# A vision tower on one core: GpSimd takes five of eight code masks and half of the high powers

## The reference, cut to what matters

```python
# the filter bank: 64 modes, 1024 times
A = jnp.exp(A_abslog + 1j * A_phase)
dtA = jnp.log(A)
Cc = (C[..., 0] + 1j * C[..., 1]) * (A - 1.0) / dtA
K = jnp.exp(dtA[:, :, None] * t)
h = 2.0 * jnp.einsum('chn,hnl->chl', Cc, K).real

# the coded weights of L0_ffn, 1024 x 1024, 16 codes, one scale for 64 of them
w = NF4_CODE[w_idx.reshape(-1, BLOCK)] * absmax[:, None]
```

## Time and profile before

| | us |
|---|---|
| median of three executions | 4150.96 |
| the profiled execution, first to last instruction | 4148.3 |
| PE busy | 3922.9 (95%) |
| DVE busy | 2708.0 (65%) |
| POOL busy | 2237.8 (54%) |
| ACT busy | 2082.5 (50%) |

### The profile page before, as it was taken

One profiled execution on the slowest core, in us unless ns is written; L12 is line 12 of the kernel. 1 busy time (PEld: TensorE's weight loads), 2 busy tenths in 40 slices (PEclk: granted clock), 3 DMA queues, 4 the chain that ended last, 5 costly groups with the idle time before them and its releaser, 6 DMA issues.

```text
span 4148.3 us, 59709 instructions
## 1 busy us (share of the span) xinstructions
PE 3922.9 (95%) x22920; PEld 2601.4 (63%) x22920; DVE 2708.0 (65%) x2970; ACT 2082.5 (50%) x3052; POOL 2237.8 (54%) x972
## 2 busy tenths in 40 slices
PE   4899999999999999999999999999999999999998
PEld 1568777444768777544577867644477877744466
DVE  6855562999355474699635565499825556389943
ACT  7842344777232344777423234577623224477732
POOL 0023343999533343799733334499843343389962
PEclk7999999999999999999999999999999999999999
DMA  4242233000322223100222223300133223300022
GB/s 111 78 147 77 82 111 108 16 15 15 119 92 82 72 87 124 58 15 15 69 102 97 77 71 120 100 13 16 40 106 97 77 87 102 110 30 15 18 84 71
DMA packets 93817, 303.28 MB, mean 73 GB/s; under 512 B 11520, under 2 KB 15872, under 8 KB 91008
## 3 DMA queue, kind: packets, MB, share of 16 engines
q1 hardware_dynamic: 80320, 275.70, 20.8%
q10 hardware_dynamic: 13248, 24.12, 1.8%
HBM read 255.74 MB, written 44.04 MB: 72 GB/s over the span
## 4 chain that ended last, share of the span: by engine, by line
PE 35%; issue 33%; DVE 20%; POOL 11%; ACT 1%; POOLq 0%; ACTq 0%; DVEq 0%
PE psg L954 20%; DVE sb_wst L1765 17%; POOL sb_wl L528 9%; PE psx L1203 4%; PE psg L1024 3%; POOL sb_wst L567 2%; PE psg L1219 2%; PE psg L1029 1%; PE psx L1251 1%; DVE psg L1738 1%; PE psg L1336 1%; DVE psg L1737 1%; PE psx L971 0%; PE psx L1274 0%; PE psx L1275 0%
## 5 line engine op out<-in xcount | busy, mean ns | idle before, releaser
L528 POOL TENSOR_TENSOR sb_wl<-sb_raw,sb_wh 128x1024 fp32r<-128x1024 f32 x388 | 961.6, 2482 | 1832.0 <-ACT sb_wh L648 1831.7
L1765 DVE TENSOR_TENSOR_SCAN sb_wst<-sb_dA,psx 128x1024 f32<-128x1024 f32 x512 | 1130.1, 2267 | 8.4 <-PE psx L1203 6.1
L790 ACT ACTIVATE sb_dA<-sb_dlt,sb_a_sb 128x504 f32<-128x504 f32 x1024 | 647.0, 705 | 53.0 <-DVE sb_wst L1765 50.8
L648 ACT ACTIVATE sb_wh<-sb_raw 128x1024 fp32r<-128x1024 f32 x388 | 407.3, 1053 | 526.0 <-PE psg L954 219.4
L1203 PEld LDWEIGHTS psx<-sb_dgB,sb_duT 64*128 64x128 f32 x4096 | 359.5, 188 | 462.1 <-DVE sb_wst L1765 322.8
L1203 PE MATMUL psx<-sb_dgB,sb_duT 64*128 64x256 f32 x4096 | 587.1, 406 | 50.1 <-DVE sb_wst L1765 48.5
L1219 PE MATMUL psg<-sb_wst,sb_cst 64*64 64x512 f32 x4096 | 607.2, 618 | 17.3 <-POOL sb_wst L567 16.4
L567 POOL TENSOR_TENSOR sb_wst<-sb_wst,sb_cb_hi 128x1024 f32<-128x1024 f32 x256 | 596.0, 2363 | 29.2 <-DVE sb_wst L1765 29.1
L567 POOL TENSOR_TENSOR sb_wst<-sb_wst,sb_cb_lo 128x1024 f32<-128x1024 f32 x256 | 600.6, 2370 | 9.8 <-DVE sb_wst L1765 9.6
L954 PE MATMUL psg<-sb_xh,sb_wh 128*128 128x512 f32 x2080 | 533.4, 398 | 12.9 <-POOL sb_wl L528 7.4
L954 PE MATMUL psg<-sb_xh,sb_wl 128*128 128x512 f32 x2080 | 515.9, 390 | 0.0
(11 more groups left out here) (283 smaller groups left out, 5059.8 us busy)
## 6 DMA issues: line engine op xcount, KB each, us to landing
sb_raw<-in_w SPq DMA_DIRECT2D x360, 512.0 KB, 3.5
sb_raw<-w_ffn_dequantized SPq DMA_DIRECT2D x32, 512.0 KB, 3.3
gates<-sb_gt ACTq DMA_DIRECT2D x64, 256.0 KB, 2.1
sb_gin<-gates SPq DMA_DIRECT2D x64, 256.0 KB, 2.7
h_after_tok<-sb_h SPq DMA_DIRECT2D x4, 2048.0 KB, 8.7
sb_h<-h_after_tok SPq DMA_DIRECT2D x4, 2048.0 KB, 8.0
out<-sb_h SPq DMA_DIRECT2D x4, 2048.0 KB, 7.2
sb_dqi<-in_w_idx ACTq DMA_DIRECT2D x28, 256.0 KB, 4.2
```

The source lines that it names most:

```text
L528: pool.tensor_tensor(rest(b, i0), raw[:, i0 % RAW, :, :], high(b, i0).bitcast(F32), ALU.subtract).then_inc(s_wl, 1)
L648: A(high(b, i0), raw[:, i0 % RAW, :, :], ACT.Copy).then_inc(s_wh, 1)
L790: ins_ = A(dA[:, (m * NQ + k) % RING, :, n, 1:S], dlt[:, m % 2, :].rearrange("p (b s) -> p b s", b=NB)[:, :, 1:S], ACT.Exp, scale=a_sb[:, ...
L1765: v.tensor_tensor_scan(wst[:, x, 4 * j:4 * j + 4, :, :].rearrange("p b n s -> p (b n s)"), dA[:, x, 4 * j:4 * j + 4, :, :].rearrange("p b ...
```

## The change

GpSimd gets a program of its own in the opening. It makes five of the eight masks of every half (`mkp`, four buffers, one compare each), VectorE two and ScalarE one. GpSimd also makes the four imaginary instructions of `high_` for every group (`high_im`), and `filters(g)` waits for them through `s_ph`. `EARLY` goes from 9 to 14, and the last two halves stand behind filter groups 0 and 1. On VectorE the table's first product now comes ahead of the first masks, and masks stand in the middle of `reduce_turns` too. The loads of codes move from ScalarE's queue to SP's, into the loop that stores the weights. ScalarE keeps two buffers for its masks and one for `away`. Strips 0 and 1 are loaded once the last low powers are made and split ahead of the last group's copies of `hT`; GpSimd makes their rests as soon as all halves are done. To free the space, `dqa` moves within SBUF.

```diff
-RING_ACT, RING_DVE = 3, 4
+RING_ACT, RING_DVE, RING_POOL = 2, 4, 4
-EARLY = 9
-LATE = [[9], [10], [11], [12], [13], [14], [15], []]
-BY_ACT = [4 if i < EARLY else 3 for i in range(HALVES)]
-BY_DVE = [PAIRS - n for n in BY_ACT]
+EARLY = 14
+LATE = [[14], [15], [], [], [], [], [], []]
+BY_DVE, BY_POOL, BY_ACT = 2, 5, 1
...
@@ sync
             for i in range(HALVES):
                 m, q = i // 2, i % 2
+                if i + 2 < HALVES:
+                    sp.wait_ge(s_dqf, i + 1)
+                    load_codes(sp, i + 2)
                 sp.wait_ge(s_dq, i + 1)
...
-            sp.wait_ge(s_hT, S // 2)
+            sp.wait_ge(s_px, S // FG)
...
                         first_strips(0, 0, 2)
+                        sp.wait_ge(s_hT, S // 2)
...
@@ gpsimd
+            def masks(i):
+                pool.wait_ge(s_dqf, i + 1)
+                for j in range(BY_POOL):
+                    at = i * BY_POOL + j
+                    if at >= RING_POOL:
+                        pool.wait_ge(s_usedp, at - RING_POOL + 1)
+                    pool.tensor_scalar(mkp[:, at % RING_POOL, :, :], dqf[:, i % 2, :, :], C("code", BY_DVE + j, 1), None,
+                                       ALU.is_equal).then_inc(s_mkp, 1)
+
+            def high_im(g):
+                a, z = g * FG, (g + 1) * FG
+                pool.wait_ge(s_tab, TAB_COEF)
+                if g >= 2:
+                    pool.wait_ge(s_filt, (g - 1) * FG // 2)
+                for blk in range(NBLK):
+                    ins_ = pool.tensor_tensor(high_[:, g % 2, 1, :, blk, :, :],
+                                              coef[:, 1, a:z, blk * NB:(blk + 1) * NB].unsqueeze(2).to_broadcast([P, FG, KC, NB]),
+                                              tabs[:, 1, a:z, 4:12].unsqueeze(3).to_broadcast([P, FG, KC, NB]), ALU.mult)
+                ins_.then_inc(s_ph, 1)
+
+            for i in range(EARLY):
+                masks(i)
+            for g in range(S // FG):
+                high_im(g)
+                for i in LATE[g]:
+                    masks(i)
+            pool.wait_ge(s_dq, HALVES)
...
@@ scalar, converted
                 if i >= 2:
-                    act.wait_ge(s_mkd, DVE0[i - 1])
+                    act.wait_ge(s_mkd, BY_DVE * (i - 1))
+                    act.wait_ge(s_mkp, BY_POOL * (i - 1))
                 A(dqf[:, q, :, :], dqi[:, q, :, :], ACT.Copy).then_inc(s_dqf, 1)
-                if i + 2 < HALVES:
-                    act.wait_ge(s_dqf, i + 1)
-                    load_codes(act, i + 2)
...
             for g in range(S // FG):
                 for i in LATE[g]:
                     masks(i)
+                if g == S // FG - 1:
+                    act.wait_ge(s_px, S // FG)
+                    act.wait_ge(s_ph, S // FG)
+                    for i in range(2):
+                        split(0, i)
                 copies(g)
...
@@ tensor, filters
                 pe.wait_ge(s_px, g + 1)
+                pe.wait_ge(s_ph, g + 1)
...
@@ vector
-            def reduce_turns(dst, ang, tmp, cols):
+            def reduce_turns(dst, ang, tmp, cols, between=None):
...
                 own.link(stt(dst, tmp, -TURN_HI, ang, ALU.mult, ALU.add))
+                if between is not None:
+                    masks(between)
...
-            masks(0)
             own.link(tt(reg, ph.unsqueeze(2).to_broadcast([P, S, 32]),
                         C("t32").unsqueeze(1).to_broadcast([P, S, 32]), ALU.mult))
-            reduce_turns(tab[:, 0, :, :], reg, reg2, 0)
+            masks(0)
+            reduce_turns(tab[:, 0, :, :], reg, reg2, 0, 1)
...
@@ vector, powers
-                for e in range(2):
-                    for blk in range(NBLK):
-                        tt(high_[:, g % 2, e, :, blk, :, :],
...
+                for blk in range(NBLK):
+                    tt(high_[:, g % 2, 0, :, blk, :, :],
```

More of the change, by code:

```diff
@@ L135 @@
 FG = 8
-EARLY = 9
-LATE = [[9], [10], [11], [12], [13], [14], [15], []]
-BY_ACT = [4 if i < EARLY else 3 for i in range(HALVES)]
-BY_DVE = [PAIRS - n for n in BY_ACT]
-ACT0 = [sum(BY_ACT[:i]) for i in range(HALVES + 1)]
-DVE0 = [sum(BY_DVE[:i]) for i in range(HALVES + 1)]
+EARLY = 14
+LATE = [[14], [15], [], [], [], [], [], []]
+BY_DVE, BY_POOL, BY_ACT = 2, 5, 1
+assert BY_DVE + BY_POOL + BY_ACT == PAIRS
 def pair_parts(p):
@@ L601, in masks @@
                 act.wait_ge(s_dqf, i + 1)
[L602 to L606, removed]
+                for j in range(BY_ACT):
+                    at = BY_ACT * i + j
+                    if at >= 1:
+                        act.wait_ge(s_mka, at)
+                    A(away[:, :, :], dqf[:, q, :, :], ACT.Abs, bias=C("minus", BY_DVE + BY_POOL + j, 1)).then_inc(s_away, 1)
                     act.wait_ge(s_away, at + 1)
@@ L609, in masks @@
                         act.wait_ge(s_useda, at - RING_ACT + 1)
-                    A(mka[:, at % RING_ACT, :, :], away[:, at % 2, :, :], ACT.Relu, bias=C("one"), scale=-1.0).then_inc(s_mka, 1)
+                    A(mka[:, at % RING_ACT, :, :], away[:, :, :], ACT.Relu, bias=C("one"), scale=-1.0).then_inc(s_mka, 1)
             def copies(g):
@@ L635, in _ @@
             A(gco[:, 2, :], mode[:, 0, :], ACT.Exp).then_inc(s_tabA, 1)
-            for i in range(5, EARLY):
+            for i in range(7, EARLY):
                 masks(i)
@@ L676, in _ @@
                         mean_copy(0)
-                    for i in range(AHEAD if b else 2):
-                        split(b, i)
+                    if b:
+                        for i in range(AHEAD):
+                            split(b, i)
                     norm(b, 0)
@@ L1414, in masks @@
                     weights(i - 2)
-                for j in range(BY_DVE[i]):
-                    at = DVE0[i] + j
+                for j in range(BY_DVE):
+                    at = BY_DVE * i + j
                     if at >= RING_DVE:
@@ L1452, in _ @@
             reduce_turns(tabs[:, 0, :, :], reg[:, :, 0:12], reg2[:, :, 0:12], 2)
+            masks(5)
             reduce_turns(tabs[:, 1, :, 0:4], reg[:, :, 0:4], reg2[:, :, 0:4], 3)
@@ L1455, in _ @@
             assert own.n == TAB_SIN[2], own.n
-            masks(3)
+            masks(6)
             for t, col in ((0, 2), (1, 4)):
@@ L1477, in _ @@
             assert own.n == TAB_E, own.n
-            masks(4)
+            masks(7)
             v.wait_ge(s_tabA, 6)
@@ L1482, in _ @@
                 own.link(tt(tab[:, t, :, :], tab[:, t, :, :], etab[:, :, :], ALU.mult))
+            masks(8)
             for t in range(2):
                 own.link(tt(tabs[:, t, :, :], tabs[:, t, :, :], etabs[:, :, :], ALU.mult))
-            masks(5)
             v.wait_ge(s_tabA, 7)
@@ L1509, in _ @@
                 own.link(stt(g2, gim, C("gmix", 4 * e + 3, 1), g2, ALU.mult, ALU.add))
-            masks(6)
+            masks(9)
             v.wait_ge(s_x, 64)
@@ L1521, in _ @@
                 own.link(tt(coef[:, e, :, :], coef[:, e, :, :], x, ALU.add))
-            masks(7)
+                masks(10 + e)
+            assert own.n == TAB_COEF, own.n
             def powers(g):
@@ L1546, in _ @@
             powers(0)
-            masks(8)
+            for i in range(12, EARLY):
+                masks(i)
             for g in range(S // FG):
```

64 lines of the change are left out of this document (36 added, 28 removed).

## The result

| | before | after |
|---|---|---|
| median beside each other, us | 4150.99 (4146.23 to 4151.47) | 4262.41 (4259.99 to 4264.87, 4 runs) |
| profiled span | 4148.3 | 4262.9 |
| first filters | 139.15 | 238.01 |
| mean starts | 232.60 | 340.64 |
| first matmul with `xh` | 242.44 | 348.59 |

The ratio is 1.0267 [1.0254, 1.0279]: slower by 2.7%, against 0.8% forecast and an upper end of 4215. All but some 8 us of the difference of the spans (114.6) is there when the first matmul with `xh` begins (106.15). The rest appears later, in instructions that the change doesn't touch. That later part takes 3902.8 to 3914.4 us in the profiled runs of this document, whatever was edited ahead of it, so a single span can't tell 10 us.

What follows compares the result with a forecast made beforehand. Mask making bounds the first stretch, TensorE the second; with VectorE and GpSimd taking turns, the mean starts 36.9 us later and the strips give -4.0: 4148.3 + 32.9 + 2.7 = 4184 us, slower by 0.8%, range 4120 to 4215.

Steps and rivals of the forecast that it cites:

- VectorE's and GpSimd's turns: Opening: instructions of the two engines exclude each other for their whole length, hiding only 0.13 to 0.14 us at a turn.
- GpSimd's mask: Opening: one GpSimd compare of 128x1024 takes 1.10 us, with ends 0.9 and 2.36.
- a sign of being wrong: GpSimd masks whose minimum is above 1.5 us would show the prediction wrong.
- Until the filters begin: From 13.3 us: GpSimd's turns 68, VectorE 78, waits 7, then products 4.6, so filters(0) starts at 171 us.
- Groups 0 and 1: First two filter groups: the fifth mask waits for TensorE until after the filters, so 19.3 us each, where now 12.
- Groups 2 to 7: Later filter groups: GpSimd's 4.6 and VectorE's 5.7 us make 10.3 each, above TensorE's 7.17.
- SP's loads at nothing: Codes' loads on SP's queue are hidden by two dqi buffers and a pace above 10 us a half.
- TensorE's clock: Opening and filters: costed at nothing, up to +10 us if the clock falls in the filters.
- The strips: First norm: strips 0 and 1 split ahead let it end at 246.1 instead of 250.1, -4.0 us.
- Slow compares: Rival: GpSimd's compare takes 1.9 to 2.36 us, 80 cost 64 to 100 more: 4245 to 4285 us; chance 0.13.
- Side by side: Rival: GpSimd's masks and products neither hold VectorE nor are held, filters(0) at 138: 4127 us; chance 0.20.
- Masks free, products in turn: Rival: only the products take turns, filters(0) at 139, no change: 4149 us; chance 0.15 for masks free or nearly so.

Runs made afterwards that it cites:

- the copies: The changed kernel with GpSimd's five masks a half made by plain copies of the same tile in place of compares: 4190.21 us.
- The forms: Two probes of the changed kernel, each making GpSimd's five masks a half by five different instructions: 4233.84 and 4194.95 us.
- strips_only: The kernel before with strips 0 and 1 loaded and split ahead of the last filters' copies, nothing else: 4151.90 us, 1.0010.
- masks_7_0_1_act: The changed kernel with seven masks on VectorE, none on GpSimd, one on ScalarE, and the codes' loads back on ScalarE's queue: 4171.88 us.
- forms1: The changed kernel with GpSimd's masks as column compare, column multiply, constant compare, copy and two-tensor product, all on 128x1024 bf16: 4233.84 us.
- forms_b: The changed kernel with GpSimd's masks as half-size compare, half-size f32 multiply, constant multiply, constant maximum and memset: 4194.95 us.

## Why the prediction was wrong

**VectorE's and GpSimd's turns.** That they collide is right: compares of 474 to 1397 ns on VectorE, a 1.93 us L1479 and a 2.01 us L1480 beside 1.23 in the earlier trace rows. That an instruction holds the place as a whole fits the copies and products, not GpSimd's scalar form. The timeline of the first masks, VectorE's and GpSimd's rows of it:

```profile
13.37 7.76 POOL L537 TENSOR_SCALAR sb_mkp<-sb_dqf,sb_cst 128x1024 bf16<-128x1024 bf16 x2 [12.92 <-ACT sb_dqf L625]
...
14.95 1.27 DVE L1478 TENSOR_SCALAR sb_wrk<-sb_wrk,sb_cst 128x2048 f32<-128x2048 f32 x1
...
16.26 1.93 DVE L1479 TENSOR_SCALAR sb_wrk<-sb_wrk 128x2048 f32<-128x2048 f32 x1
...
18.23 2.01 DVE L1480 TENSOR_SCALAR sb_wrk<-sb_wrk 128x2048 f32<-128x2048 f32 x1
```

L1478 passes in its usual time inside the first compare, which runs from 13.37 to 17.11; L1479, across that compare's end, ends 0.7 us late. L1480 lies inside the second compare (17.10 to 21.14) and still takes 2.01. That compare takes 4.04 us, as if it had got under way only when L1479 ended at 18.19, and then L1480 met its start. I read this as a compare that holds VectorE up near its start and near its end, and lets it through between. The Trainium skill, page "SBUF — State Buffer", section "Who interferes with whom", has it as an exclusive lock for the whole instruction, and lets VectorE's `tensor_scalar` in its two-port modes take part. That such forms take part agrees with L1479; L1478's 1.27 us inside a compare does not agree with a hold from start to end. That the hold lies in reading and in writing, with the instruction's own work between, is argued from these rows and not shown.

**GpSimd's mask.** This is the step that failed: "I take 1.10", with ends 0.9 and 2.36. It measured 2.83 at its fastest, above even the upper end and above the 1.5 us that the prediction named as a sign of being wrong. I had divided the time of a two-input instruction by its reads, as if the elements read set it. The forms show that this holds for a copy (1.04) and not for any scalar operation tried (2.76 to 2.85). The estimate of 0.85 us plus a fixed part (up to 0.19) by the Trainium skill's page "GPSIMD Engine Reference", section "Engine selection" ("1-input is roughly line-rate"), agrees with the copy's 1.04 and not with the compare's 2.83.

**Until the filters begin.** With the right price the form of the sum fails too. I added GpSimd's time and VectorE's (68 + 78 + 7); with 2.83 us it would put `filters(0)` at 292 (13.3 + 189 + 78 + 7 + 4.6), and 238.0 was measured. GpSimd's 70 masks of 3.15 us and its four products are the whole stretch, and VectorE's work lies beneath. Of the 3.15, 2.83 are the instruction and 0.32 the turns. With the copies the sum stood within 5 us: 171 forecast, 165.8 and 166.1 measured.

**Groups 0 and 1.** Forecast 19.3, measured 21.4 and 20.6, by another mechanism. GpSimd's timeline:

```profile
237.84 11.30 POOL L537 TENSOR_SCALAR sb_mkp<-sb_dqf,sb_cst 128x1024 bf16<-128x1024 bf16 x4
250.20 4.13 POOL L537 TENSOR_SCALAR sb_mkp<-sb_dqf,sb_cst 128x1024 bf16<-128x1024 bf16 x1 [1.06 <-PE psx L951]
254.30 4.99 POOL L547 TENSOR_TENSOR sb_high<-sb_coef,sb_tabs 128x512 f32<-128x512 f32 x4
```

The fifth mask waits 1.06 us for TensorE, not 7, because the four before it take 11.30 us while the filters run. The masks and products fill the group by themselves. With the copies, where my mechanism could work, the groups took 19.6 to 20.4.

**Groups 2 to 7**: forecast 10.3 each, measured (340.6 - 280.0) / 6 = 10.1. The turns are as forecast, with a median of 1.55 us for VectorE's products beside GpSimd's, where the earlier trace rows have 0.68. That the number fits so well is in part luck. The sum had VectorE and GpSimd fill the group, but they work in pairs of groups of 20.6 us, in which VectorE still waits 1.68 us for the first filters of the pair (310.19). Those took 9.4 us (300.76 to 310.19) in place of 7.17, the granted clock being 0.87 in this stretch.

**SP's loads at nothing** was right on the whole, in every pair that differs in the loads alone, to within 7 us. "If the masks were done every 5 us it would show": nowhere were they.

**TensorE's clock** I costed at nothing, with up to 10 us. At 0.67 in the opening it cost nothing that shows, as TensorE waited. After it, the first two filter groups took 10.0 and 9.6 us for 7.2, beneath GpSimd's compares. At the handover it shows in the open, below.

**The strips** were put at -4.0. That step failed too: they bring nothing, as the run with the strips alone shows. The prediction had the splits "go where both engines wait for TensorE", and ScalarE waits for the loads instead, with the last copies of `hT` queued behind it. ScalarE's rows in the change:

```profile
336.30 2.24 ACT L657 ACTIVATE sb_wh<-sb_raw 128x1024 fp32r<-128x1024 f32 x2 [5.38 <-DMA sb_raw<-in_w]
338.44 2.05 ACT L649 ACTIVATE sb_hT<-psg 128x512 f32<-128x512 f32 x4
```

TensorE waits 3.47 us for these copies ahead of the mean, where it was 0.78. The way from the mean to the first `xh` matmul fell from 9.8 to 8.0 us only, and with the strips alone from 9.8 to 6.9. No 2.47 us `xl` is left, as forecast:

```profile
348.90 0.68 DVE L1620 TENSOR_TENSOR sb_xl<-sb_xc,sb_xh 128x512 fp32r<-128x512 f32 x1
```

And TensorE's clock was down. From the mean to the first `xh` matmul, the windows of the change, of strips_only and of masks_7_0_1_act:

```profile
340.60:348.60 8.00, 5.72 (x19) 1.21 (x19) 1.50 (x3) 2.58 (x4) 1.49 (x1) 0.50 0.92 330
```

```profile
233.30:240.20 6.90, 4.65 (x19) 0.97 (x19) 1.50 (x3) 2.53 (x4) 1.43 (x1) 0.75 0.92 322
```

```profile
251.30:256.60 5.30, 3.06 (x19) 0.81 (x19) 1.50 (x3) 2.54 (x4) 1.46 (x1) 0.97 0.97 371
```

At a granted clock of 0.50, 0.75 and 0.97 the same work takes 8.0, 6.9 and 5.3 us. The splits put a gap of 3.47, 4.44 and 3.24 us ahead of the mean in these three runs, and in two of them the clock is low behind it. The gap's length alone doesn't decide: behind 3.43 us in forms1 the mean's matmuls took 3.64 us, behind 3.50 us in forms_b 1.92. What does isn't shown.

**The rivals.** *Slow compares* (4245 to 4285, chance 0.13) is what happened. Its time holds by luck, by two errors that cancel: its price stopped at 2.36, and at 2.83 us its rule of 80 times the excess would give 4184 + 80 x 1.73 = 4322. The 60 us between that and the measured time are VectorE's work that lies beneath GpSimd's and that the sum had added to it. *Side by side* fell: with copies, where GpSimd's work is short, VectorE was busy 142 us and not the 94 that its own work comes to. *Masks free, products in turn* fell with it.

## What to carry to other kernels

Before work goes to an engine that does nothing, price the very form of instruction there by one probe run. A price scaled from another form of the same engine was off by a factor of 2.6, outside the range that I had called bounds. Two engines that share a place came close to adding up where both were busy (the copies), and the larger alone counted where the other had slack (the compares); so find the crossing (here between three and four masks), and take a shared place's cost from a run in which both are busy (1.07 us a mask, not 0.68). And look first at what the busy engine waited for: moving one mask of eight from ScalarE to VectorE in the nine early halves, with the strips ahead, won some 11 us, where 80 masks on the idle engine cost 95 of 111. Work that is moved ahead onto an engine with a fixed order also holds up what stands behind it, when its data come late.

## What was not expected of the hardware

- GpSimd: an operation with a scalar on 128x1024 bf16 takes 2.76 to 2.85 us, the product of two bf16 tensors 1.89, a copy 1.04, a memset 0.95. The scalar form costs 2.5 ns an element and 0.3 us fixed, and f32 input is no dearer (1.49 us for 512 against 1.57).
- Beside GpSimd's compares, VectorE's scalar forms of 128x2048 f32 stretch from 1.23 to 1.93 and 2.01 us, while its form with a scalar and two tensors (L1481, L1484) keeps 2.29. Beside GpSimd's copies L1481's form takes 3.0 and L1484's 3.1 (L1483 in that kernel):

```profile
L1483 DVE SCALAR_TENSOR_TENSOR sb_tab<-sb_wrk,sb_tab 128x2048 f32<-128x2048 f32 x2 | 6.2, 3114 | 0.0
```
